# Cross-attention and quantised feed-forward on one core: probabilities in 64-column chunks, the rests as 32-row tiles

## The chip, the cores and the metric

The kernel runs on one core of a Trainium2 chip. The metric is device microseconds of one execution, the median of three runs. Engines are named as the profile names them: PE multiplies matrices (PEld is its weight load), DVE, ACT and POOL work elementwise, SP issues DMAs.

## The reference, cut to what matters

```python
x = x + attention(layernorm(x), ctx, Wq, Wk, Wv, Wo, bo)     # x (8, 512, 512), ctx (8, 77, 384)
x = x + ffn(layernorm(x), clip_x, clip_h, w_gate, w_up, w_down)

def attention(x, c):               # 8 heads of 64, L = 77 context rows
    q, k, v = split(x @ Wq), split(c @ Wk), split(c @ Wv)
    attn = softmax(einsum('bhsd,bhld->bhsl', q, k) * 64 ** -0.5)
    return merge(einsum('bhsl,bhld->bhsd', attn, v)) @ Wo + bo

def ffn(x):                        # one scale for the whole of x, one for the whole of h, one per weight row
    xq = fake_quant(x, clip_x)
    h = fake_quant(silu(xq @ quant(w_gate).T) * (xq @ quant(w_up).T), clip_h)
    return h @ quant(w_down).T
```

Because the scale of x is a maximum over all rows, no row enters the feed-forward part before attention has ended for all of them.

## The kernel before, in words

There are eight batches of 512 rows (index b) and 32 tiles of 128 rows (index n or s, s = 4b + t). The first stage is attention, and beside it the weights of the feed-forward part are turned into integers. The second and third stages are the two feed-forward products; the change touches neither.

Each engine has one queue. The order of calls in the code is the order in each queue, and each call names tokens (semaphore and value) that its engine waits for; nothing behind a waiting instruction of that engine starts before it. Matrix products of the attention stage that need more than bfloat16 split each operand into a high and a low part and add three products, high by high, high by low, low by high, of 32-bit words ("f32" in the rows). So one product over 128 contraction rows is three PE instructions of 512 columns.

`attend(s)` is one step of the loop over tiles. In it stand, for different tiles: `S(s+1)`, the scores, eight PE instructions into the two SP banks; `soft_max`, `soft_sub` (DVE), `soft_exp` (ACT), `soft_sum`, `soft_rec` (DVE) and `soft_norm` (POOL), the softmax of tile s+1, which leaves probabilities of 8 heads x 77 columns = 616 columns in `P`, a ring of three; `PT(s)`, five transposes of 128 columns to the PTP banks, then `PT_high` (ACT) and `PT_low` (DVE), which leave the transposed probabilities, high and low, in `pts` as five chunks of 128 contraction rows by 512; `wo(s-5)`, twelve PE instructions of the output product into the bank WOP, and `residual(s-5)` (DVE), which reads WOP and adds x; `second_stats`, `second_aggr`, `second_scale`, `normed` and `largest`, the second layernorm and the running maximum; `first_stats(s+3)` to `first_bias(s+3)`, the first layernorm's figures; `q_chunk`, twelve PE instructions each, four chunks a batch, which use the two QO banks in turn.

One feed-forward weight tile goes through each step: `w_load(s)` (SP, into `wraw`, two buffers), `w_top(s-1)` (a DVE maximum), `w_scale`, `w_inverse`, `w_round(s-1)` (ACT), `w_integer(s-1)` (POOL), `w_turn(s-2)` (PE transposes into the bank MI) and `w_out(s-2)` (ACT, out of MI). `w_turn` waits for the last reader of MI, whose token is `t_we["last"]`.

Every fourth step (t = 0, b >= 1) also holds the product of probabilities and V of batch b-1, `PV(b-1, j)` for the head pairs j = 0..3. Heads of 77 rows don't line up with chunks of 128, so a pair of heads meets two chunks: there are eight blocks (chunk, pair), listed in `BLOCKS`, each 128 rows by 128 columns of V in `vbd` with zeros where the other head's rows lie. PV(b, j) is six PE instructions into a QO bank, and one ACT and one DVE instruction (L200, L202) read the bank and leave the high and low part in `os_`. `load_vb(b)` fills `vbd` for batch b from a scratch in HBM in twelve DMAs on SP. It waits for the last PV of the batch before (`t_PV`). It stands in attend(4b), behind the store of x1 and the load of x, ahead of everything that attend(4b+1) issues on SP.

The order of a step with t = 0 is written out by hand (L659 to L697): `first_stats`, `w_top`, `first_aggr`, `w_scale`, `wo`, `residual`, `w_inverse`, PV 0, second statistics, PV 1, S, `soft_max`, `soft_sub`, PV 2, `soft_exp`, PT, `largest`, `soft_sum`, `soft_rec`, PV 3, `load_vb`, `PT_high`, `PT_low`. After the loop the last batch's PV comes behind `wo(27)` and `residual(27)` (L861 to L872), and `wo(28)` to `wo(31)` follow, each head pair of `wo(28)` as soon as its part of `os_` is there.

Of the kernel before, what the change touches and what calls it, by code (L numbers as in the profile page):

```python
# [54 lines left out]
def block_kernel(nc, x, xT, ctxT, Wq, Wk, Wv, Wo, bo, clip_x, clip_h, w_gate, w_up, w_down, out):  # L55
    f32, f32r, bf16 = mybir.dt.float32, mybir.dt.float32r, mybir.dt.bfloat16
    ALU, ACT, AX = mybir.AluOpType, mybir.ActivationFunctionType, mybir.AxisListType
    NB, L, H, D, I = 8, 77, 8, 512, 1408
    NT, NI = 32, 11
    HL = H * L  # L60
# [5 lines left out]
    with ctx:  # L66
# [75 lines left out]
        UR = 3  # L142
        P = sb(late, "P", [128, UR, 640])
        qs = sb(late, "qs", [128, 2, 4, 512])
# [5 lines left out]
        n2 = sb(late, "n2", [128, RR, D])  # L150
        vbd = sb(late, "vbd", [128, 2, 8, 128], f32r)
        pts = sb(late, "pts", [128, 2, 5, 512], f32r)
# [171 lines left out]
        t_bn1, t_q, t_oss, t_st2, t_wmx, t_wsc = [Tokens() for _ in range(6)]  # L324

        def q_chunk(b, m):
            w = slice(m * 128, m * 128 + 128)
            pairs = [(wqs[:, 0, k, w], wqs[:, 1, k, w], xTs[:, 0, k, :], xTs[:, 1, k, :])
                     for k in range(4)]
            at, bank, t_qh[b, m] = qo_bank(pairs, 512, 128, [*t_wql, *t_xTs[b]])  # L330
            t_q[b] = copy("act", qs[:, b % 2, m, :], bank,
                          [t_qh[b, m], t_S.get(4 * (b - 2) + 3), t_ctxl, *t_wql], "q_out")
            state["free"][at] = (t_q[b],)

        BLOCKS = [(0, 0), (1, 0), (1, 1), (2, 1), (2, 2), (3, 2), (3, 3), (4, 3)]

        def load_vb(b):
            at = 0
            while at < HL:
                hh, l0, ch, p0 = at // L, at % L, at // 128, at % 128  # L340
                n = min(L - l0, 128 - p0)
                blk = BLOCKS.index((ch, hh // 2))
                t = dma("sp", vbd[p0:p0 + n, :, blk, (hh % 2) * 64:(hh % 2) * 64 + 64],
                        vd[b * L + l0:b * L + l0 + n, :, hh * 64:hh * 64 + 64],
                        [t_v[(b * L + L - 1) // 128], t_v[b * L // 128], t_PV.get(b - 1), t_vb["zero"]], "ld_vb")
                at += n
            t_vb[b] = t
# [23 lines left out]
        def soft_sub(n):  # L371
# [19 lines left out]
        def soft_norm(n):  # L391
            u = P[:, n % UR, 0:HL].rearrange("p (h l) -> p h l", h=H)
            rb = rs8[:, n % 2, :].unsqueeze(2).broadcast_to([128, H, L])
            t_norm[n] = add("pool", lambda e: e.tensor_tensor(u, u, rb, ALU.mult), [t_rec[n]], "sm_nrm")  # L394

        def PT(n):
            b, t = n // 4, n % 4

            def fn(e):
                for k in range(5):  # L400
                    m = e.transpose(PTP[:, k * 128:k * 128 + 128], P[:, n % UR, k * 128:k * 128 + 128],  # L401
                                    identF[:, :])
                return m
# [9 lines left out]
        def PT_low(n):  # L413
            w = slice(n % 4 * 128, n % 4 * 128 + 128)
            t_pl[n] = less("dve", pts[:, 1, :, w], PT_src, pts[:, 0, :, w], [t_ph[n]], "PT_lo")

        def PV(b, j):
            pairs = [(vbd[:, 0, i, :], vbd[:, 1, i, :], pts[:, 0, ch, :], pts[:, 1, ch, :])
                     for i, (ch, jj) in enumerate(BLOCKS) if jj == j]
            last = qo_product(pairs, 512, 128, [t_pl[4 * b + 3], t_vb[b]], lambda bank: [  # L420
                (bank, os_[:, 0, j, :], os_[:, 1, j, :])], [t_Wo.get(4 * b - 1)] + t_flat)
            t_oss[b, j] = last[1]
            t_PV[b] = ("qo_mm", c.count["qo_mm"])

# [202 lines left out]
        def attend(s):  # L627
# [31 lines left out]
            if t == 0:  # L659
# [14 lines left out]
                if s > 0:
                    S(s + 1)
                    soft_max(s + 1)
                    soft_sub(s + 1)
# [492 lines left out]
```

How the kernel before makes its waits and increments, by code:

```python
    def run(self, engine, e):  # L39
        for need, fn, sem, by in self.queue[engine]:
            for s, v in need:
                e.wait_ge(s, v)
            ins = fn(e)
            if sem is not None:
                ins.then_inc(sem, by)
```

## Time and profile before

| what | us |
|---|---|
| median of three runs | 599.78 (599.04 to 600.22) |
| profiled execution, its own time | 599.7 |
| its span | 597.9 |
| PE busy in the span | 560.9 |
| DVE busy in the span | 492.2 |
| attention stage, from the start to about | 328 |

The profiled execution's own time is 1.8 us over its span, and 0.1 us under the median. A PE instruction's end in the profile is modelled, 0.39 us after the start for 512 columns, while the next one starts 0.23 us after it: starts are to be read, not busy time.

### The profile page before, as it was taken

To read this page: it belongs to the slowest core of one execution; us is meant where nothing else is said; L and a number is where in the kernel's file an instruction comes from. 1 tells how busy PE (TensorE), PEld (TensorE's weight loads), DVE (VectorE), ACT (ScalarE), POOL (GpSimd) and SP (SyncE) were. 2 spreads that over 40 slices of the span, in tenths; PEclk is the share of its full clock that TensorE was granted. 3 is DMA by queue.
4 is the path that set the end of the run, shared out by engine and by line. 5 is a ranking of instruction groups with operands and counts; after the bars stand their busy time and mean duration, and the time that the engine had idled before them with its cause. 6 is when DMAs were issued, how large, how long until landed. Compare 5 with 4: busy or idle time off the path is not lost.

```text
span 597.9 us, 8609 instructions
## 1 busy us (share of the span) xinstructions
PE 560.9 (94%) x2919; PEld 381.9 (64%) x2943; DVE 492.2 (82%) x873; ACT 327.5 (55%) x466; POOL 254.6 (43%) x321
## 2 busy tenths in 40 slices
PE   4999799999999999999989899999999999778996
PEld 2987578888888888888878644444444446333342
DVE  3747876888979797887986699889988988899994
ACT  4743456456665655655342566656665635993210
POOL 3656847658576585755532000000000000476764
PEclk9999899999999999999999999999999999999999
DMA  8617254846466573625257906532020200299975
GB/s 321 217 70 268 62 168 136 273 116 192 167 210 233 161 214 118 210 72 182 81 182 285 345 18 265 197 138 72 1 70 2 70 2 1 84 289 323 325 246 175
DMA packets 68476, 98.04 MB, mean 164 GB/s; under 512 B 31977, under 2 KB 31977, under 8 KB 67921
## 3 DMA queue, kind: packets, MB, share of 16 engines
q1 hardware_dynamic: 68429, 97.50, 49.2%
q8 instruction: 23, 0.38, 0.3%
q14 instruction: 20, 0.16, 0.1%
q10 hardware_dynamic: 4, 0.00, 0.0%
HBM read 59.70 MB, written 37.78 MB: 163 GB/s over the span
## 4 chain that ended last, share of the span: by engine, by line
PE 61%; issue 11%; DVE 11%; DMA 7%; POOL 4%; SPq 3%; ACT 2%; DVEq 0%; POOLq 0%; ACTq 0%
PE SP L972 10%; PE QO L972 10%; PE QO L183 7%; PE QO L185 6%; PE QO L184 6%; PE SP L356 4%; SPq L37 3%; PE WOP L435 3%; PE WOP L437 3%; PE WOP L436 3%; POOL n2b L1090 3%; DMA out<-n2b 2%; DVE wgu L1049 2%; PE PTP L401 2%; DVE wgu L1058 2%
## 5 line engine op out<-in xcount | busy, mean ns | idle before, releaser
L1090 POOL TENSOR_TENSOR n2b<-n2b 128x512 f32<-128x512 f32 x31 | 54.0, 1757 | 208.3 <-DVE n2b L1088 208.3
L972 PE MATMUL SP<-nT,wgu 128*128 128x512 bf16 x345 | 89.8, 379 | 0.4
L972 PE MATMUL QO<-nT,wgu 128*128 128x512 bf16 x343 | 88.7, 379 | 1.2 <-ACT nT L210 0.8
L978 ACT ACTIVATE sil<-QO,fsc 128x512 f32<-128x512 f32 x88 | 60.7, 689 | 50.5 <-PE QO L972 44.9
L982 DVE SCALAR_TENSOR_TENSOR h<-SP,fsc,sil 128x512 f32<-128x512 f32 x88 | 65.9, 749 | 14.9 <-PE SP L972 14.9
L394 POOL TENSOR_TENSOR P<-P,rs 128x616 f32<-128x616 f32 x32 | 39.0, 1219 | 73.7 <-DVE rs L388 73.6
L1046 ACT ACTIVATE h<-h,magic,g 128x1536 f32<-128x1536 f32 (+2 forms) x38 | 48.7, 1365 | 28.1 <-DMA h<-h_spill 24.4
L985 DVE TENSOR_REDUCE hmx<-h 128x1 f32<-128x512 f32 x88 | 60.4, 686 | 3.0
L972 PEld LDWEIGHTS SP<-nT,wgu 128*128 128x128 bf16 x352 | 34.4, 98 | 41.5
L183 PE MATMUL QO<-xTs,wqs 128*128 128x512 f32 x128 | 52.5, 410 | 4.2 <-POOL xTs L214 2.7
L972 PEld LDWEIGHTS QO<-nT,wgu 128*128 128x128 bf16 x352 | 33.2, 98 | 35.4 <-ACT nT L210 0.7
L185 PE MATMUL QO<-xTs,wqs 128*128 128x512 f32 x128 | 50.8, 397 | 0.0
L184 PE MATMUL QO<-xTs,wqs 128*128 128x512 f32 x128 | 50.5, 394 | 0.0
L435 PE MATMUL WOP<-wos,os 128*128 128x512 f32 x116 | 46.4, 400 | 0.0
L437 PE MATMUL WOP<-wos,os 128*128 128x512 f32 x116 | 45.3, 391 | 0.0
L436 PE MATMUL WOP<-wos,os 128*128 128x512 f32 x116 | 45.2, 389 | 0.0
L379 ACT ACTIVATE P<-P,r 128x616 f32<-128x616 f32 x32 | 26.0, 812 | 33.2 <-DVE P L375 33.1
L456 POOL TENSOR_TENSOR xn<-xn,bob 128x512 f32<-128x512 f32 x32 | 41.3, 1295 | 0.0
L356 PE MATMUL SP<-kst,qs 128*128 128x154 f32 x256 | 39.9, 298 | 0.3 <-DVE P L375 0.3
L544 ACT ACTIVATE wraw<-wraw,magic,wiv 128x512 f32<-128x512 f32 (+1 forms) x26 | 24.3, 933 | 28.5 <-DVE wiv L537 28.5
L200 ACT ACTIVATE os<-QO 128x512 fp32r<-128x512 f32 x32 | 19.2, 599 | 36.8 <-PE QO L185 36.8
L1058 DVE TENSOR_SCALAR wgu<-wgu 128x1536 bf16<-128x1536 bf16 (+2 forms) x39 | 37.4, 973 | 0.0
(163 smaller groups left out, 1265.4 us busy)
## 6 DMA issues: line engine op xcount, KB each, us to landing
xTr<-in_xT SPq DMA_DIRECT2D x8, 1024.0 KB, 6.8
xn<-in_x SPq DMA_DIRECT2D x32, 256.0 KB, 4.0
x_rows<-x SPq DMA_DIRECT2D x32, 256.0 KB, 3.2
n_rows<-n SPq DMA_DIRECT2D x32, 256.0 KB, 2.5
n2b<-n_rows SPq DMA_DIRECT2D x32, 256.0 KB, 4.1
n2b<-x_rows SPq DMA_DIRECT2D x32, 256.0 KB, 4.2
out<-n2b SPq DMA_DIRECT2D x32, 256.0 KB, 3.2
h_spill<-h SPq DMA_DIRECT2D x2, 2816.0 KB, 9.6
```

What stands on the lines that cost most here:

```text
L183: e.matmul(ps, lh, rh, start=(i == 0), stop=False)
L184: e.matmul(ps, lh, rl, start=False, stop=False)
L185: m = e.matmul(ps, ll, rh, start=False, stop=(i == n - 1))
L356: m = e.matmul(o, qs[:, b % 2, j, w], kst[:, b, j, :], start=(j % 2 == 0), stop=True, skip_group_check=True)
L435: e.matmul(wo_bank(n), os_[:, 0, j, w], wos[:, 0, j, :], start=(j == 0), stop=False)
L436: e.matmul(wo_bank(n), os_[:, 0, j, w], wos[:, 1, j, :], start=False, stop=False)
L437: return e.matmul(wo_bank(n), os_[:, 1, j, w], wos[:, 0, j, :], start=False, stop=(j == 3))
L972: m = e.matmul(ps, wv_[:, k, col:col + 128], nT[:, b % 2, k, :], start=(k == 0), stop=(k == 3))
L978: t_sil[n] = add("act", lambda e: e.activation(sil[:, n % SR, :], gp, ACT.Silu, scale=fsc[:, ic:ic + 1]), [t_g[n], t_fs, t_h.get(n - SR)] ...
L982: t_h[n] = add("dve", lambda e: e.scalar_tensor_tensor(out=hv, in0=up, scalar=fsc[:, 11 + ic:12 + ic], in1=sil[:, n % SR, :], op0=ALU.mult ...
L985: t_hm[n] = add("dve", lambda e: e.tensor_reduce(hmx[:, n:n + 1], hv, AX.X, ALU.max, apply_absolute_value=True), [t_h[n]], "hmx")
L1090: t_oa[m] = add("pool" if m < NT - 1 else "dve", lambda e: e.tensor_tensor(xo[:, so, :], xo[:, so, :], xo[:, m % 4, :], ALU.add), [t_om[m] ...
```

## The change

What it does:

- The normalised probabilities no longer overwrite `P`; `soft_norm` writes them to a new tile `PN`, two buffers of 640 columns, in two POOL instructions: columns 0 to 63 of each head at pitch 64 (four chunks of 128, one for each head pair), and the other 13 of each head at pitch 16 (the fifth chunk: 32 rows for each head pair).
- `vbd` has five blocks: four of 128 rows (one for each head pair) and one in which head pair j has rows 32j to 32j+31. `load_vb` issues two DMAs a head, sixteen in all.
- The product is a new function `PV_rest(b)`, twelve PE instructions with 32 contraction rows each, the four head pairs in turn, into four banks (the two QO banks, MI, WOP), and then `PV(b, j)` with three PE instructions of 128 rows that add to bank j. `PV_rest` waits for the four banks: the two QO ones, the last reader of MI, and `residual(4b-1)` as the reader of WOP.
- The reader of head pair 2's bank becomes `t_we["last"]`, for which the next `w_turn` waits. `wo(n)` of the first tile of a batch waits for all four parts of `os_` before its first instruction.
- In a step with t = 0, S, `soft_max` and `soft_sub` go ahead of `PV_rest` and PV 0, `soft_exp` behind PV 0, `soft_sum` and `soft_rec` ahead of PV 3, and PT and `largest` behind PV 3.

```diff
-        P = sb(late, "P", [128, UR, 640])
+        P = sb(late, "P", [128, UR, HL])
+        PN = sb(late, "PN", [128, 2, 640])
-        vbd = sb(late, "vbd", [128, 2, 8, 128], f32r)
+        vbd = sb(late, "vbd", [128, 2, 5, 128], f32r)
...
+        M0 = 64
+        M1 = L - M0
         def load_vb(b):
...
+            for hh in range(H):
+                c0, j = hh % 2 * 64, hh // 2
+                for p0, blk, l0, l1 in ((c0, j, 0, M0), (16 * hh, 4, M0, L)):
+                    t = dma("sp", vbd[p0:p0 + l1 - l0, :, blk, c0:c0 + 64],
+                            vd[b * L + l0:b * L + l1, :, hh * 64:hh * 64 + 64], waits, "ld_vb")
...
         def soft_norm(n):
-            rb = rs8[:, n % 2, :].unsqueeze(2).broadcast_to([128, H, L])
-            t_norm[n] = add("pool", lambda e: e.tensor_tensor(u, u, rb, ALU.mult), [t_rec[n]], "sm_nrm")
+            for at, l0, l1, pitch in ((0, 0, M0, 64), (512, M0, L, 16)):
+                to = PN[:, n % 2, at:at + H * pitch].rearrange("p (h l) -> p h l", h=H)[:, :, 0:l1 - l0]
+                rb = rs8[:, n % 2, :].unsqueeze(2).broadcast_to([128, H, l1 - l0])
+                t_norm[n] = add("pool", lambda e, to=to, rb=rb, l0=l0, l1=l1: e.tensor_tensor(
+                    to, u[:, :, l0:l1], rb, ALU.mult), [t_rec[n], t_PT.get(n - 2), t_pz], "sm_nrm")
...
+        def PV_rest(b):
+            banks = []
+            for j in range(2):
+                at = state["use"] % 2
+                state["use"] += 1
+                banks.append((at, state["banks"][at], state["free"][at]))
+            banks.append((None, MI[:, :], (t_we["last"], *t_dgs[1:])))
+            banks.append((None, WOP[:, :], (t_x1.get(4 * b - 1),)))
+            pv_at[b] = banks
+            def fn(e):
+                for i, (hv, hp) in enumerate(((0, 0), (0, 1), (1, 0))):
+                    for j in range(4):
+                        q = slice(32 * j, 32 * j + 32)
+                        m = e.matmul(banks[j][1], vbd[q, hv, 4, :], pts[q, hp, 4, :], start=(i == 0), stop=False)
+                return m
+            add("pe", fn, [t_pl[4 * b + 3], t_vb[b], *(t for bank in banks for t in bank[2])], "qo_mm")
+
         def PV(b, j):
+            at, bank, _ = pv_at[b][j]
+            def fn(e):
+                e.matmul(bank, vbd[:, 0, j, :], pts[:, 0, j, :], start=False, stop=False)
+                e.matmul(bank, vbd[:, 0, j, :], pts[:, 1, j, :], start=False, stop=False)
+                return e.matmul(bank, vbd[:, 1, j, :], pts[:, 0, j, :], start=False, stop=True)
+            t_PV[b] = add("pe", fn, [], "qo_mm")
...
+            if j < 2:
+                state["free"][at] = (t_oss[b, j],)
+            elif j == 2:
+                t_we["last"] = t_oss[b, j]
...
-                t_Wo[n] = add("pe", fn, [t_oss[b, j], t_wol, free, t_c], "Wo_mm")
+                t_Wo[n] = add("pe", fn, [t_oss[b, 3 if t == 0 else j], t_wol, free, t_c], "Wo_mm")
...
                 when("w", w_inverse, s - 1)
+                if s > 0:
+                    S(s + 1)
+                    soft_max(s + 1)
+                    soft_sub(s + 1)
+                when("pv", PV_rest, b - 1)
                 when("pv", PV, b - 1, 0)
+                if s > 0:
+                    soft_exp(s + 1)
                 when("wo", second_stats, s - 5)
                 when("wo", second_aggr, s - 5)
                 when("wo", second_scale, s - 5)
                 when("pv", PV, b - 1, 1)
                 when("pv", PV, b - 1, 2)
+                when("s", soft_sum, s + 1)
+                when("s", soft_rec, s + 1)
+                when("pv", PV, b - 1, 3)
...
                 PT(s)
                 when("am", largest, s - 7)
-                when("s", soft_sum, s + 1)
-                when("s", soft_rec, s + 1)
-                when("pv", PV, b - 1, 3)
...
         second_stats(27)
+        PV_rest(7)
         PV(7, 0)
```

## Rows read from the trace of the kernel before

**Rows 1.** The page, its first part: busy time, share of span, instructions.

```profile
PE 560.9 (94%) x2919; PEld 381.9 (64%) x2943; DVE 492.2 (82%) x873; ACT 327.5 (55%) x466; POOL 254.6 (43%) x321
```

**Rows 2.** Busy time by window: PE, PEld, DVE, ACT, POOL, granted clock, DMA share.

```profile
182.40:217.00 34.60, 34.52 (x192) 29.13 (x192) 30.41 (x60) 20.66 (x32) 23.39 (x34) 1.00 0.62 196
```

**Rows 3.** Waits, attention stage: engine, line, releaser, us in total, times, longest.

```profile
DVE wmx L528 <- DMA wraw<-in_ffn_w_gate: 10.5, 4, 3.0
```

**Rows 4.** Timeline 181.5 to 193, PE and PEld: start, us (merged), instruction.

```profile
182.44 0.39 PE L183 MATMUL QO<-pts,vbd 128*128 128x512 f32 x1
182.66 0.39 PE L184 MATMUL QO<-pts,vbd 128*128 128x512 f32 x1
...
184.93 1.20 PEld L356 LDWEIGHTS SP<-kst,qs 128*128 128x128 f32 x8
185.16 1.21 PE L356 MATMUL SP<-kst,qs 128*128 128x154 f32 x8
186.10 0.49 PE L183 MATMUL QO<-pts,vbd 128*128 128x512 f32 x1
...
187.60 0.71 PE L401 MATMUL PTP<-identF,P 128*128 128x128 f32 x5
...
189.54 0.40 PE L564 MATMUL MI<-identB,wint 128*128 128x128 bf16 x4
```

**Rows 5.** The same timeline, DVE and ACT around residual(11) and PV.

```profile
182.44 0.69 DVE L442 BATCH_NORM_STATS2 bn<-xn 128x6 f32<-128x512 f32 x1 [0.69 <-DMA xn<-in_x]
...
183.86 0.69 DVE L461 TENSOR_TENSOR x<-WOP,xn 128x512 f32<-128x512 f32 x1
...
184.00 0.60 ACT L200 ACTIVATE os<-QO 128x512 fp32r<-128x512 f32 x1 [1.32 <-PE QO L185]
...
184.63 0.69 DVE L202 TENSOR_TENSOR os<-QO,os 128x512 fp32r<-128x512 f32 x1
...
185.23 0.68 DVE L467 BATCH_NORM_STATS2 bn<-x 128x6 f32<-128x512 f32 x1
...
185.95 0.18 DVE L471 BATCH_NORM_AGGREGATE mv<-bn 128x2 f32<-128x6 f32 x1
186.05 0.66 DVE L202 TENSOR_TENSOR os<-QO,os 128x512 fp32r<-128x512 f32 x1
...
186.63 0.79 DVE L368 TENSOR_REDUCE mx<-SP 128x8 f32<-128x616 f32 x1
```

**Rows 6.** The tile vbd: duration ns min/median/max, first and last start.

```profile
L37 SPq DMA_DIRECT2D vbd<-v_halves x96: 613/795/955, 64.1 to 302.0; - x96
```

**Rows 7.** Timeline of SP: V loads and the weight load behind them.

```profile
64.13 9.86 SPq L37 DMA_DIRECT2D vbd<-v_halves  x12
...
189.77 9.79 SPq L37 DMA_DIRECT2D vbd<-v_halves  x12
...
200.77 0.65 SPq L37 DMA_DIRECT2D wraw<-in_ffn_w_up  x1
```

**Rows 8.** Timeline of DVE, from w_top(17) to residual(15).

```profile
204.14 0.69 DVE L528 TENSOR_REDUCE wmx<-wraw 128x1 f32<-128x512 f32 x1 [2.76 <-DMA wraw<-in_ffn_w_up]
...
206.62 0.69 DVE L461 TENSOR_TENSOR x<-WOP,xn 128x512 f32<-128x512 f32 x1 [0.83 <-PE WOP L437]
...
218.63 0.69 DVE L461 TENSOR_TENSOR x<-WOP,xn 128x512 f32<-128x512 f32 x1
```

**Rows 9.** Timeline, the first PV and what DVE waits for there.

```profile
75.74 0.47 PE L183 MATMUL QO<-pts,vbd 128*128 128x512 f32 x1 [0.97 <-DMA vbd<-v_halves]
...
77.50 0.69 DVE L528 TENSOR_REDUCE wmx<-wraw 128x1 f32<-128x512 f32 x1 [3.03 <-DMA wraw<-in_ffn_w_gate]
```

**Rows 10.** Timeline, the steps in which batch 6 and batch 7 get their PV.

```profile
287.08 0.69 DVE L461 TENSOR_TENSOR x<-WOP,xn 128x512 f32<-128x512 f32 x1
...
293.81 0.49 PE L435 MATMUL WOP<-wos,os 128*128 128x512 f32 x1
...
311.68 0.69 DVE L461 TENSOR_TENSOR x<-WOP,xn 128x512 f32<-128x512 f32 x1 [1.08 <-PE WOP L437]
...
317.30 0.39 PE L435 MATMUL SP<-wos,os 128*128 128x512 f32 x1
```

More of the change, by code:

```diff
@@ L324, in block_kernel @@
         t_bn1, t_q, t_oss, t_st2, t_wmx, t_wsc = [Tokens() for _ in range(6)]
+        t_dgs = []
         def q_chunk(b, m):
@@ L333, in q_chunk @@
             state["free"][at] = (t_q[b],)
-        BLOCKS = [(0, 0), (1, 0), (1, 1), (2, 1), (2, 2), (3, 2), (3, 3), (4, 3)]
+        M0 = 64
+        M1 = L - M0
         def load_vb(b):
[L338 to L346, printed above, removed]
+            waits = [t_v[(b * L + L - 1) // 128], t_v[b * L // 128], t_PV.get(b - 1), t_vb["zero"]]
+            for hh in range(H):
[3 more added lines that the diff above has]
+                            vd[b * L + l0:b * L + l1, :, hh * 64:hh * 64 + 64], waits, "ld_vb")
             t_vb[b] = t
@@ L375, in soft_sub @@
             t_sub[n] = add("dve", lambda e: e.tensor_tensor(u, S4, mb, ALU.subtract),
-                           [t_mx[n], t_PT.get(n - UR), t_wkl, t_ctxl], "sm_sub")
+                           [t_mx[n], t_norm.get(n - UR), t_wkl, t_ctxl], "sm_sub")
         def soft_exp(n):
@@ L400, in fn @@
                 for k in range(5):
-                    m = e.transpose(PTP[:, k * 128:k * 128 + 128], P[:, n % UR, k * 128:k * 128 + 128],
+                    m = e.transpose(PTP[:, k * 128:k * 128 + 128], PN[:, n % 2, k * 128:k * 128 + 128],
                                     identF[:, :])
@@ L415, in PT_low @@
             t_pl[n] = less("dve", pts[:, 1, :, w], PT_src, pts[:, 0, :, w], [t_ph[n]], "PT_lo")
-        def PV(b, j):
[L418 to L423, printed above, removed]
+        pv_at = {}
+        def PV_rest(b):
[14 more added lines that the diff above has]
+            add("pe", fn, [t_pl[4 * b + 3], t_vb[b], *(t for bank in banks for t in bank[2])], "qo_mm")
+        def PV(b, j):
+            at, bank, _ = pv_at[b][j]
[4 more added lines that the diff above has]
+            t_PV[b] = add("pe", fn, [], "qo_mm")
+            hi, lo = os_[:, 0, j, :], os_[:, 1, j, :]
+            waits = [t_Wo.get(4 * b - 1)] + t_flat
+            th = add("act", lambda e: e.activation(hi, bank, ACT.Copy), [t_PV[b], *waits], "qo_hi")
+            t_oss[b, j] = add("dve", lambda e: e.tensor_tensor(lo, bank, hi.bitcast(f32), ALU.subtract),
+                              [th, *waits], "qo_lo")
+            if j < 2:
+                state["free"][at] = (t_oss[b, j],)
+            elif j == 2:
+                t_we["last"] = t_oss[b, j]
         def wo_bank(n):
@@ L431, in wo @@
             w = slice(t * 128, t * 128 + 128)
-            free = t_x1.get(n - 1) if n < 28 else (t_sub[31], None, t_x1[27], t_pl[31])[n - 28]
+            free = t_x1.get(n - 1) if n < 28 else (t_sub[31], None, t_oss[7, 3], t_pl[31])[n - 28]
             for j in range(4):
@@ L597, in block_kernel @@
         t_wol = less("pool", wos[:, 1], wor[:, :, :], wos[:, 0], [t_woh], "wo_lo")
-        t_pz = add("pool", lambda e: e.memset(P[:, :, HL:640], 0.0), [t_ctxl, t_wkl], "c_pz")
+        t_pz = add("pool", lambda e: e.memset(PN[:, :, 512:640], 0.0), [t_ctxl, t_wkl], "c_pz")
         v_rows(0)
@@ L673, in attend @@
                 when("pv", PV, b - 1, 1)
[L674 to L677, printed above, removed]
                 when("pv", PV, b - 1, 2)
-                if s > 0:
-                    soft_exp(s + 1)
+                when("s", soft_sum, s + 1)
+                when("s", soft_rec, s + 1)
+                when("pv", PV, b - 1, 3)
                 if big:
```

1 line of the change is left out of this document (removed).

## The prediction, made before the changed kernel ran

> **What bounds the kernel now.** I read the page's busy times first [rows 1]: PE 560.9 of 597.9 us. Busy PE time is modelled, so I went to a window of one batch in the attention stage [rows 2]: PE 34.5 of 34.6 us, DVE 30.4, at full clock (1.00, the 2.4 GHz level). The timeline by starts says the same [rows 4]: 512-column products start 0.227 us apart without a gap. PE sets the pace of this stage, and a batch's PV is 24 such starts, 24 x 0.227 = 5.45 us. The waits then show what lies close behind PE [rows 3]: DVE waits 10.5 us in four times for weight tiles, and for the other weight another three times. In each batch one `w_top` stands idle 2.5 to 2.8 us [rows 8], because its load leaves SP only behind the twelve V loads, 9.8 us of issuing [rows 7]. So DVE has some 4 us of idle time a batch, and nearly three of them hang on SP, not on PE.
>
> **The change part by part.** I call G the end of the residual that releases WOP: 183.86 + 0.69 = 184.55 for s = 16 [rows 5].
>
> *PE work.* 24 starts become 12 full ones, 12 x 0.227 = 2.72 us, and 12 with 32 rows, which I call R. No row shows tiles of 32 rows. Below: the four banks' tiles run together, three slots, 3 x 0.227 = 0.7 us. Above: they run one by one with a hand-over at each end, 2.72 + 0.2 = 2.9 us (the hand-over is the 0.33 against 0.23 us by which a product after scores starts late, in the same timeline). Between lies the weight load: the scores load 128 columns of 32-bit weights for each of eight instructions and start 0.94/8 = 0.118 us apart with far fewer columns to stream [rows 4]. Twelve tiles bring twelve such loads, 12 x 0.118 = 1.4 us. I take 1.4, since it is the only row with as many loads for as little streaming. PE alone would then save 5.45 - 2.72 - 1.4 = 1.3 us a batch.
>
> The Trainium skill (TensorE: Matmul & The Clock Gate, measured speedup of packing) gives 3.07 times for four tiles of 32 rows and 512 columns; by that R would be 2.72/3.07 = 0.9, an estimate, and the sum about 3.5 us lower. Its page TensorEngine Tiling (Array Packing), key properties, says that a change of tiling mode drains the array, which speaks against the change at both ends of the twelve. No row of this trace shows either.
>
> *The new wait for WOP.* `PV_rest` waits for G. Before, PV began at 182.44, as soon as wo(11) had been issued [rows 4]. Now scores fill 0.95 us of it, to 183.39, and then PE stands until 184.61: 1.2 us. Residual is late because DVE has `first_stats` (0.69 us waiting for x), `w_top` and two small ones in front of it [rows 5]. G minus the start of PV in the six batches with a residual is 3.3, 1.6, 2.1, 1.35, 0.9 and 2.1 us, and 0.9 at the end, where nothing fills it. Behind the waiting instruction on PE stand all of PV, PT, `w_turn` and the next scores.
>
> *The new wait for MI.* `w_turn` now waits for the DVE reader of head pair 2. From the start of PV 0: 0.84 to its third product's end, 0.04 and 0.60 for ACT, 0.03, so DVE's first reader starts at 1.51; then by starts 0.60, 0.72, 0.10 (reader, statistics, aggregate), 0.58, and the third reader's 0.69 [rows 5] with a handover: about 4.3 us, while PE needs 2.72 + 0.55 for the rest of PV and PT. So `w_turn` starts at G + 0.06 + R + 4.3 = G + 5.8, here 190.3, against 189.54 before. PE's saving of 1.3 has become a loss of 0.8 us in this batch.
>
> *Four more V loads.* Issue time hardly depends on the rows of a piece: 0.61 to 0.96, median 0.80 us [rows 6]; a piece of 25 rows takes 0.72. Four more at 0.72 are 2.9 us; low end 1.7 (all sixteen like the shortest kinds), high end 3.4. SP's next weight load goes out so much later, and DVE already waits for it.
>
> *One batch round.* From G to the next G by way of SP and DVE, at s = 16: 0.06 + R 1.4 + 2.72 + 0.21 to PV's end (4.39); V loads and what follows to the landing of the weight tile, 204.14 - 189.77 = 14.37 before [rows 7, 8], plus 2.9; DVE from `w_top` to the next residual's end, 219.32 - 204.14 = 15.18 less the 0.83 us in which it waits for PE [rows 8], which vanish: 14.35. Sum 36.0, before 219.32 - 184.55 = 34.8: +1.2. The other four rounds repeat the pattern with their own figures: s = 8 to 12, 36.2 against 34.3, +1.9; 12 to 16, 36.3 against 35.8, +0.5; 20 to 24, 35.2 against 34.8, +0.4; 24 to 28, which has fewer q products, 33.1 against 33.6, -0.5. There PE's own way, 0.06 + 1.4 + 4.3, then 25.3 us of PE work unchanged, then 2.1, gives the same 33.1. Together +3.5 us.
>
> *The first PV.* PE already waits 0.97 us for V [rows 9]: twelve issues from 64.13 [rows 7] set it. With sixteen V is there 2.9 us later, about 78.7, and the weight tile behind them too, so that `w_top` starts near 80.5 instead of 77.50 [rows 9]. `soft_max` and `soft_sub` now stand between it and the readers: they end about 83.2, the third reader about 85.9, and `w_turn`, at 82.91 before, starts at 86: +3.0 us. The scores moved ahead only fill a wait.
>
> *The last two.* At s = 28 there is no `w_turn`, but wo(24) waits for all four readers. With sum and reciprocal ahead of the fourth it is G + 0.06 + 1.4 + 5.8 = 295.0 (G = 287.77) against 293.81 [rows 10]: +1.2. After the loop: G = 312.37; PV 0 at 313.8, first reader 315.3, then aggregate, two readers, `largest`, the fourth until 318.5; wo(28) at 318.6 against 317.30 [rows 10]: +1.3. Before, nine products of wo(28) covered the last reader; now nothing does.
>
> *At nothing.* `soft_norm` in two POOL instructions costs at most some 0.1 us each time; POOL has 11 us free a batch [rows 2], and PT comes a step later. Zeroing is shorter. S moved ahead: its softmax comes earlier, nobody waits for it. The three-deep `P` is released earlier, which nobody needed. If POOL's cover were gone, 32 x 0.1 = 3 us.
>
> **Sum.** 3.0 + 3.5 + 1.2 + 1.3 = +9.0 us. On the profiled execution's 599.7 (span 597.9 and 1.8 around it) that is 608.7; the median of the runs shown is 0.1 above that execution.
>
> **The rivals.**
>
> *The saving comes through (faster).* Place: the wait for WOP. If residual kept pace, because PE's waits give DVE time to catch up, and the V loads' issue stayed hidden, each of eight PVs would keep 2.72 - 1.4 = 1.3 us: 599.7 - 10.5 = 589.2. It decides where G comes within 0.95 us of the end of wo, as in one batch of seven. Against it: DVE's wait for the weight tile [rows 8] is in its own queue and grows with SP's work whatever PE does.
>
> *Cheap tiles, cheap issues (no change).* R = 0.7 and 1.7 us for the V loads. Then PE's way binds: rounds +0.7, -0.5, 0, -0.7, -1.2, first PV +1.8, last two +0.5 and +0.6, in sum +1.2: 600.9.
>
> *The tiles don't run together.* The change doesn't do what it says, R = 2.9. Each of the five rounds and the last two get 1.5 longer, the first hardly: 608.7 + 10.5 = 619.2. For it: no row shows tiles side by side. Against: they go to different banks and different rows.
>
> **How the numbers follow.** Forecast 55%, its own range 604 to 613 (R from 0.9 to 2, issues 2.4 to 3.4 us). Saving 14%, cheap 17%, one by one 14%. Less than 0.2% (1.2 us) can't be told from no change. Cheap splits evenly over faster, same and slower; faster 0.19, same 0.07, slower 0.74. The range 598 to 619 leaves out most of the saving case and the top of the one-by-one case.
>
> **What would show it.** Right: the twelve 32-row tiles spanning about 1.4 us; PE idle before them, released by the residual; PE idle before `w_turn`, released by the DVE reader; sixteen V issues of 12.7 us; DVE's four waits for the one weight, 10.5 us [rows 3], grown to over 16; a batch round near 36 us; PE idle of 1 to 2 us before wo(28). Wrong: tiles in under 0.8 us, a residual that ends within a microsecond of wo, DVE waits for weight tiles as before, or a batch round under 34 us.

## The result, and the profile after

| | median us | lowest to highest | profiled span | mean granted clock |
|---|---|---|---|---|
| before | 599.41 | 598.66 to 600.22 | 597.9 | 0.996 |
| after | 609.85 | 609.62 to 610.27 | 608.3 | 0.988 |

The changed kernel is slower: ratio 1.0175, 95% interval 1.0157 to 1.0192. The span grew by 10.4 us; the forecast was +9.0, 608.7 us.

The page of after, busy times first (answers to [rows 1]). PE is busy 1.8 us less in a span that is 10.4 us longer, so its share fell from 94% to 92%: what PE was spared, and more, came back as waits (and a stretch at half the clock, below, counts as busy).

```profile
PE 559.1 (92%) x2943; PEld 372.6 (61%) x2943; DVE 491.7 (81%) x873; ACT 324.1 (53%) x466; POOL 258.7 (43%) x353
```

The waits of after between 20 and 355 us (engine, line, releaser, total us, times, longest) name the new ones: `w_turn` waits for the reader that frees MI, `PV_rest` for the residual that frees WOP, wo(28) (bank SP) and wo(24) (bank WOP) for the fourth reader. DVE still waits for weight tiles, 11.1 us in three times where [rows 3] had 10.5 in four.

```profile
PE MI L599 <- DVE os L453: 7.7, 6, 3.2
PE QO L438 <- DVE x L496: 4.8, 6, 2.1
...
PE SP L470 <- DVE os L453: 1.9, 1, 1.9
PE WOP L470 <- DVE os L453: 1.3, 1, 1.3
...
DVE wmx L563 <- DMA wraw<-in_ffn_w_gate: 11.1, 3, 4.9
DVE wmx L563 <- DMA wraw<-in_ffn_w_up: 9.7, 3, 3.3
```

One batch's PV at s = 16, from the timeline of after (start, us, instruction), stands against [rows 4, 5]. The first four tiles, in four banks, start within 0.01 us of each other, and so do their weight loads. The next fours start 0.30 to 0.34 and 0.23 us later, and the first full product 0.32 to 0.36 after the last four: R = 192.63 - 191.73 = 0.90 us. Then 12 products, PT, and PE stands until the third reader (196.26 + 0.68) has freed MI.

```profile
190.89 0.69 DVE L496 TENSOR_TENSOR x<-WOP,xn 128x512 f32<-128x512 f32 x1
...
191.73 0.50 PE L438 MATMUL QO<-pts,vbd 32*128 32x512 f32 x2 [0.18 <-DVE x L496]
191.74 0.18 PEld L438 LDWEIGHTS MI<-pts,vbd 32*128 32x128 f32 x1
191.74 0.49 PE L438 MATMUL MI<-pts,vbd 32*128 32x512 f32 x1
191.74 0.18 PEld L438 LDWEIGHTS WOP<-pts,vbd 32*128 32x128 f32 x1
191.74 0.49 PE L438 MATMUL WOP<-pts,vbd 32*128 32x512 f32 x1
...
192.04 0.39 PE L438 MATMUL QO<-pts,vbd 32*128 32x512 f32 x1
...
192.27 0.39 PE L438 MATMUL QO<-pts,vbd 32*128 32x512 f32 x1
...
192.63 0.50 PE L446 MATMUL QO<-pts,vbd 128*128 128x512 f32 x1
...
195.48 0.71 PE L405 MATMUL PTP<-identF,PN 128*128 128x128 f32 x5
196.26 0.68 DVE L453 TENSOR_TENSOR os<-MI,os 128x512 fp32r<-128x512 f32 x1
197.09 0.38 PE L599 MATMUL MI<-identB,wint 128*128 128x128 bf16 x4 [0.91 <-DVE os L453]
```

SP of after, then DVE of after (against [rows 7] and [rows 8]). Sixteen V loads take 12.15 us, the weight load goes out at 209.06, and DVE waits 3.10 us for its tile. The wait is hardly longer than before, although the load is later, because everything behind the V loads moved along.

```profile
195.72 12.15 SPq L37 DMA_DIRECT2D vbd<-v_halves  x16
...
209.06 0.66 SPq L37 DMA_DIRECT2D wraw<-in_ffn_w_up  x1
```

```profile
212.26 0.69 DVE L563 TENSOR_REDUCE wmx<-wraw 128x1 f32<-128x512 f32 x1 [3.10 <-DMA wraw<-in_ffn_w_up]
...
214.32 0.69 DVE L496 TENSOR_TENSOR x<-WOP,xn 128x512 f32<-128x512 f32 x1 [0.41 <-PE WOP L472]
...
226.83 0.69 DVE L496 TENSOR_TENSOR x<-WOP,xn 128x512 f32<-128x512 f32 x1
```

The first PV of after (against [rows 9]). DVE waits 4.85 us for a weight tile; `soft_max`, `soft_sub` and the readers stand behind it, and PE waits 3.24 us for MI. After that wait PE runs with starts 0.43 us apart instead of 0.23.

```profile
79.81 0.69 DVE L563 TENSOR_REDUCE wmx<-wraw 128x1 f32<-128x512 f32 x1 [4.85 <-DMA wraw<-in_ffn_w_gate]
...
85.22 0.59 PE L599 MATMUL MI<-identB,wint 128*128 128x128 bf16 x4 [3.24 <-DVE os L453]
...
88.62 0.63 PE L186 MATMUL QO<-xTs,wqs 128*128 128x512 f32 x1
...
89.05 0.63 PE L184 MATMUL QO<-xTs,wqs 128*128 128x512 f32 x1
```

Busy time of after in that stretch (PE, PEld, DVE, ACT, POOL, granted clock): the clock is 0.50, the 1.2 GHz level, for these 5.7 us, in which PE is busy all the time. I call this a slow stretch. In windows of 0.25 us it begins at 84.5, while PE still stands, and ends at about 91.4.

```profile
85.50:91.20 5.70, 5.70 (x20) 4.93 (x19) 4.92 (x8) 1.82 (x3) 3.23 (x4) 0.50 0.15 32
```

The end of the attention stage in after (against [rows 10]): PE waits for WOP, and then 1.92 us for wo(28)'s fourth reader.

```profile
321.42 0.50 PE L438 MATMUL QO<-pts,vbd 32*128 32x512 f32 x2 [0.88 <-DVE x L496]
...
327.28 0.50 PE L470 MATMUL SP<-wos,os 128*128 128x512 f32 x1 [1.92 <-DVE os L453]
```

**Where the 10.4 us came from.** I call G, as in the prediction, the end of the residual in front of a batch's PV, and add up by G. First PV and the round behind it, up to s = 8: 119.71 against 114.43, +5.3. From s = 8 to the last G: 201.57 against 197.94, +3.6. From there to the end: 287.01 against 285.54, +1.5. G is an event on DVE. After's PV waits for it; the PV of before doesn't, and there G comes 0.9 to 3.3 us behind the start of PV. So G splits the whole, but a single round of before can differ from the round that PE sees.

### The profile page after: what moved, and what is told of

It is laid out like the page before. It is cut to its first block, busy times and chain, and to the rows that moved or that the text cites. A ratio compares the mean times of both kernels' runs of the same rounds, so it can differ in the third digit from the quotient of the medians.

```text
span 608.3 us, 8706 instructions
## 1 busy us (share of the span) xinstructions
PE 559.1 (92%) x2943; PEld 372.6 (61%) x2943; DVE 491.7 (81%) x873; ACT 324.1 (53%) x466; POOL 258.7 (43%) x353
## 4 chain that ended last, share of the span: by engine, by line
PE 51%; DVE 15%; issue 13%; POOL 8%; DMA 6%; ACT 3%; SPq 3%; POOLq 0%; DVEq 0%; ACTq 0%
PE QO L1007 10%; PE SP L1007 10%; POOL n2b L1125 5%; PE QO L184 4%; PE QO L186 4%; PE QO L185 4%; SPq L37 3%; PE SP L357 3%; PE WOP L470 2%; PE WOP L471 2%; PE WOP L472 2%; DVE os L453 2%; DMA xn<-in_x 2%; DVE x L496 1%; DMA n2b<-x_rows 1%
## 5 line engine op out<-in xcount | busy, mean ns | idle before, releaser
L1007 PE MATMUL QO<-nT,wgu 128*128 128x512 bf16 x352 | 90.3, 379 | 0.6 <-ACT nT L211 0.6
L397 POOL TENSOR_TENSOR PN<-P,rs 128x512 f32<-128x512 f32 x64 | 44.2, 712 | 64.1 <-DVE rs L389 64.1
L184 PE MATMUL QO<-xTs,wqs 128*128 128x512 f32 x128 | 53.3, 417 | 4.6 <-POOL xTs L215 2.7
L186 PE MATMUL QO<-xTs,wqs 128*128 128x512 f32 x128 | 51.4, 402 | 0.0
L185 PE MATMUL QO<-xTs,wqs 128*128 128x512 f32 x128 | 51.3, 400 | 0.0
L470 PE MATMUL WOP<-wos,os 128*128 128x512 f32 x116 | 46.9, 405 | 1.3 <-DVE os L453 1.3
L471 PE MATMUL WOP<-wos,os 128*128 128x512 f32 x116 | 45.8, 395 | 0.0
L472 PE MATMUL WOP<-wos,os 128*128 128x512 f32 x116 | 45.8, 394 | 0.0
L563 DVE TENSOR_REDUCE wmx<-wraw 128x1 f32<-128x512 f32 (+1 forms) x26 | 21.0, 809 | 20.7 <-DMA wraw<-in_ffn_w_gate 11.1
L357 PEld LDWEIGHTS SP<-kst,qs 128*128 128x128 f32 x256 | 36.5, 194 | 1.6 <-DVE P L376 0.8
```

The lines of the kernel that those rows point to most:

```text
L184: e.matmul(ps, lh, rh, start=(i == 0), stop=False)
L185: e.matmul(ps, lh, rl, start=False, stop=False)
L186: m = e.matmul(ps, ll, rh, start=False, stop=(i == n - 1))
L357: m = e.matmul(o, qs[:, b % 2, j, w], kst[:, b, j, :], start=(j % 2 == 0), stop=True, skip_group_check=True)
L470: e.matmul(wo_bank(n), os_[:, 0, j, w], wos[:, 0, j, :], start=(j == 0), stop=False)
L471: e.matmul(wo_bank(n), os_[:, 0, j, w], wos[:, 1, j, :], start=False, stop=False)
```

## The experiments

The table has every run. G(8) is G at s = 8, "six rounds" goes from it to the last G (before the PV of batch 7), "rest" from there to the end of the span; these three are of the profiled execution (that of e2_mi0 took 601.8 us, at the low end of its runs). The ratio is against the kernel before on the same chip (599.62, 599.65 and 599.49 us beside e1 to e4, e5 to e8 and e9 to e12).

| kernel | V loads a batch | median us | ratio (95%) | G(8) | six rounds | rest |
|---|---|---|---|---|---|---|
| before | 12 | 599.41 | 1 | 114.43 | 197.94 | 285.54 |
| after | 16 | 609.85 | 1.0175 (1.0157 to 1.0192) | 119.71 | 201.57 | 287.01 |
| e1_v12 | 12 | 599.45 | 0.9997 (0.9987 to 1.0007) | 112.32 | 198.17 | 288.54 |
| e2_mi0 | 16 | 604.86 | 1.0084 (1.0065 to 1.0104) | 113.02 | 200.00 | 287.02 |
| e3_full | 16 | 620.63 | 1.0341 (1.0324 to 1.0359) | 116.69 | 211.90 | 290.35 |
| e4_b16 | 16 | 618.29 | 1.0309 (1.0295 to 1.0323) | 119.25 | 211.89 | 285.49 |
| e5_before_spread | 12 in four | 639.84 | 1.0662 (1.0647 to 1.0676) | 114.92 | 232.52 | 290.45 |
| e6_after_spread | 16 in four | 633.78 | 1.0569 (1.0545 to 1.0593) | 121.18 | 222.33 | 291.38 |
| e7_spread_mi0 | 16 in four | 629.93 | 1.0491 (1.0461 to 1.0521) | 116.00 | 219.89 | 292.93 |
| e8_spread_all | 16 in four | 627.07 | 1.0438 (1.0407 to 1.0468) | 112.38 | 222.99 | 289.71 |
| e9_before_half | 12 in two | 598.75 | 0.9989 (0.9980 to 0.9997) | 113.75 | 197.21 | 285.53 |
| e10_after_half | 16 in two | 603.47 | 1.0076 (1.0056 to 1.0096) | 114.65 | 197.70 | 288.57 |
| e11_half_mi0 | 16 in two | 596.02 | 0.9947 (0.9935 to 0.9959) | 112.83 | 192.52 | 288.52 |
| e12_half_all | 16 in two | 590.57 | 0.9855 (0.9842 to 0.9868) | 111.71 | 191.76 | 286.25 |

### One part at a time

**e1_v12**: the kernel after without the four loads it adds; the last 13 rows of the odd heads are left out.

```diff
-                for p0, blk, l0, l1 in ((c0, j, 0, M0), (16 * hh, 4, M0, L)):
+                for p0, blk, l0, l1 in ((c0, j, 0, M0), (16 * hh, 4, M0, L))[:2 - hh % 2]:
```

> The changed kernel with twelve V loads a batch instead of sixteen (the rests of the four odd heads are left out, so their last 13 context rows count as zero). My theory: the four extra issues are on the path of DVE (the weight tile's load stands behind them); without them the rounds shrink until PE's own way binds, some 0.9 us in each of five, and the first PV and the clock drop behind it get 2 us shorter: about 604 us. Rival, that only PE's waits for banks matter: within 1 us of 609.9.

Measured: 599.45, no difference from before, 4.6 us below the theory's 604; the rival is out. So the four loads carry the whole loss, 10.4 us, and the rest of the change comes to zero: what PE saves it gives back. The two new waits of this kernel, with the 1.93 us before wo(28), show 9.6 us of that. DVE's waits for the one weight are down to 4.1 us, 2.7 of them at the first PV:

```profile
PE MI L599 <- DVE os L453: 5.1, 6, 0.9
...
PE QO L438 <- DVE x L496: 2.6, 4, 1.1
...
DVE wmx L563 <- DMA wraw<-in_ffn_w_gate: 4.1, 4, 2.7
```

Not all of the 10.4 us is the longer block of loads itself. After's slow stretch behind the first PV, some 2.8 us (see e3_full), is missing here: the granted clock is 1.00 from 85.5 to 91.2. On the other side this kernel has a slow stretch behind wo(28) that after hasn't, in the windows of e1_v12 and then of after:

```profile
316.50:319.75 3.25, 3.25 (x8) 2.57 (x9) 0.51 (x1) 0.00 (x0) 0.00 (x0) 0.52 0.80 292
```

```profile
327.30:330.50 3.20, 3.20 (x14) 2.60 (x15) 0.64 (x2) 0.00 (x0) 0.00 (x0) 1.00 0.84 274
```

wo(28) starts 5.99 and 6.01 us after the last G in the two, but the next PE instruction that waits (L938) comes at 23.79 against 22.26. These 1.5 us are why the column "rest" is 288.5 here. e10_after_half and e11_half_mi0 have the same slow stretch and the same 1.5 us, and e3_full has it beside its longer PV. Why the clock falls there in four kernels and not in after and e2_mi0, which stand as long before wo(28), no run shows.

**e2_mi0**: MI goes to the first head pair instead of the third, so that its reader comes first.

```diff
-            banks.append((None, MI[:, :], (t_we["last"], *t_dgs[1:])))
+            banks.insert(0, (None, MI[:, :], (t_we["last"], *t_dgs[1:])))
...
-            if j < 2:
+            if 1 <= j <= 2:
                 state["free"][at] = (t_oss[b, j],)
-            elif j == 2:
+            elif j == 0:
                 t_we["last"] = t_oss[b, j]
```

> The changed kernel with MI given to head pair 0 instead of pair 2, whose DVE reader comes first, so w_turn's wait ends some 2 us earlier. If the wait for MI is on the path: PE's gap of 1.07 us before w_turn goes in five batches, the 3.4 us one at the first PV shrinks, and the half clock behind it (3 us) goes: about 600. If SP's V loads and DVE set the rounds, only the first PV and the clock get better: about 605. If neither: 609.9.

Measured: 604.86 (601.83 to 606.06), 5.0 us less than after, as the middle case had it. The parts can be read only for the profiled execution, which took 601.83, 8.2 us less than after's. Its rounds gain only 1.6 us: the wait for MI is gone, and others stand in its place, of which these are the largest.

```profile
PE QO L184 <- DVE xTs L215: 2.8, 5, 1.9
PE PTP L405 <- DVE pts L215: 2.5, 6, 1.3
PE MI L599 <- POOL wint L585: 2.1, 4, 1.1
```

The larger gain is before s = 8: G(8) is 6.7 us earlier. Its `w_turn` at the first PV starts at 82.28 instead of 85.22, after a wait of 0.54 instead of 3.24, and from 82.20 to 92.00 the granted clock stays at 1.00:

```profile
82.28 0.38 PE L599 MATMUL MI<-identB,wint 128*128 128x128 bf16 x4 [0.54 <-DVE os L453]
```

```profile
82.20:92.00 9.80, 9.72 (x57) 8.43 (x58) 9.04 (x16) 6.24 (x11) 4.64 (x6) 1.00 0.36 117
```

5.7 us at half the clock cost after about 2.85 us, an estimate; with the 2.9 by which `w_turn` is earlier that is 5.8 of the 6.7.

**e3_full**: the 12 rest tiles as full instructions of 128 rows, in four blocks of their own.

```diff
-                        q = slice(32 * j, 32 * j + 32)
-                        m = e.matmul(banks[j][1], vbd[q, hv, 4, :], pts[q, hp, 4, :], start=(i == 0), stop=False)
+                        m = e.matmul(banks[j][1], vbd[:, hv, 4 + j, :], pts[:, hp, 4, :], start=(i == 0), stop=False)
```

> The changed kernel with the twelve 32-row tiles as twelve full 128-row instructions (V's rests in four blocks with zeros), all else as it is. The tiles take 0.90 us a batch in the trace, twelve full starts would take 2.72. If PE's way is on the path: +1.8 us x 8, about 623. If the tiles' saving is hidden behind SP and DVE: under +5, below 615.

Measured: 620.63, +10.8 us over after. The twelve tiles became 2.80 to 2.85 us instead of 0.90; from first to last start a PV takes 5.32 instead of 3.53, so it is 1.8 us longer eight times, 14.3 us. A round got 1.7 us longer on average (211.90 - 201.57 over six), so a microsecond of PV is on the path nearly whole. What is missing to 14.3 lies before s = 8, where G came 3.0 us earlier than in after: here PE stands only 1.42 us before `w_turn` at the first PV, and the slow stretch of after is missing.

```profile
84.95 0.38 PE L598 MATMUL MI<-identB,wint 128*128 128x128 bf16 x4 [1.42 <-DVE os L452]
```

```profile
84.00:90.00 6.00, 5.05 (x29) 4.41 (x30) 5.93 (x9) 3.53 (x6) 3.26 (x4) 1.00 0.29 91
```

This run also prices that stretch. From `w_turn` to G at s = 8, where the two kernels do the same work behind the same sixteen loads, it takes 31.74 us (116.69 - 84.95), after 34.49 (119.71 - 85.22), before 31.5: the stretch costs after some 2.8 us.

**e4_b16**: the kernel before, with four of its pieces of 77 rows cut into 64 and 13. Same data and PE work, 16 loads.

```diff
-                t = dma("sp", vbd[p0:p0 + n, :, blk, (hh % 2) * 64:(hh % 2) * 64 + 64],
...
+                for r0, r1 in ((0, 64), (64, 77)) if n == 77 else ((0, n),):
+                    t = dma("sp", vbd[p0 + r0:p0 + r1, :, blk, (hh % 2) * 64:(hh % 2) * 64 + 64],
```

> The kernel before with four of its twelve V pieces of 77 rows cut in 64 and 13, so sixteen V loads a batch, same data. My theory: the issues cost by themselves about 2 us at the first PV, and in the rounds they only lengthen DVE's wait for the weight tile from 2.7 to 5 us, of which PE sees little, since it doesn't wait for the residual: 601.5 to 604. Rival, that the V loads alone explain the change: about 610.

Measured: 618.29, +18.7 us. This is the miss that taught most. I had taken DVE's idle time for slack of PE in the kernel before; four loads, 2.5 us of issuing, made a batch 1.4 to 3.3 us longer by G in each of five rounds, and G(8) 4.8 later. By the starts of PV on PE, the better measure for this kernel, the first two PVs are 3.0 and 6.5 us later than before, and the five rounds 1.8, 2.6, 4.1, 2.5 and 1.2 us longer: at most places no more than the 2.5 us of issuing. The 4.1 holds a slow stretch (below), and another, from 79.7 to 83 us, lies in the first PV behind a wait of 2.58 us for V. SP of this kernel, the w_top behind it, and its waits:

```profile
200.66 12.24 SPq L37 DMA_DIRECT2D vbd<-v_halves  x16
...
214.13 0.64 SPq L37 DMA_DIRECT2D wraw<-in_ffn_w_up  x1
```

```profile
217.49 0.69 DVE L530 TENSOR_REDUCE wmx<-wraw 128x1 f32<-128x512 f32 x1 [5.21 <-DMA wraw<-in_ffn_w_up]
...
233.11 0.69 DVE L463 TENSOR_TENSOR x<-WOP,xn 128x512 f32<-128x512 f32 x1 [0.82 <-PE WOP L439]
```

```profile
PE PTP L403 <- DVE pts L214: 5.4, 6, 1.2
...
DVE wmx L530 <- DMA wraw<-in_ffn_w_gate: 21.4, 5, 5.8
DVE wmx L530 <- DMA wraw<-in_ffn_w_up: 15.5, 3, 5.2
```

The late weight tile makes `w_top` late, with it everything behind it on DVE, and in the fourth step `PT_low`, for which PE's next PT waits. In the round from s = 16 PE stands 1.16, 0.35 and 0.23 us there, and behind these short waits the granted clock is 0.50 from about 226.5 to 229.8:

```profile
224.05 0.74 PE L403 MATMUL PTP<-identF,P 128*128 128x128 f32 x5 [1.16 <-DVE pts L214]
```

```profile
226.50:229.75 3.25, 3.25 (x9) 2.48 (x9) 3.22 (x9) 0.69 (x1) 3.09 (x5) 0.50 1.00 307
```

`w_top` to G takes 1.1 us longer than before in this round, and 0.2 longer in the one ahead of it, which has no slow stretch. One round, from G at s = 16 to the next, split alike in three kernels (before from [rows 5, 7, 8]):

| | G to first V issue | V issues | to w_top | w_top to next G | round |
|---|---|---|---|---|---|
| before | 5.22 | 9.79 | 4.58 | 15.18 | 34.77 |
| e4_b16 | 4.96 | 12.24 | 4.59 | 16.31 | 38.10 |
| after | 4.13 | 12.15 | 4.39 | 15.26 | 35.93 |

So a ring runs through all three: PV, V loads (they wait for PV), weight tile, DVE, PV. In after its last link is the residual, for which `PV_rest` waits. In before and e4_b16 PV doesn't wait for the residual, and the last link is `PT_low`, for which PT waits. In e4_b16 the ring sets the rounds. In before PE does (PE waits 0.2 us in all for `PT_low`, and e9_before_half below loosens the ring without gain), but the ring has almost nothing to spare, so that 2.5 us of issuing came through whole. After is 8.4 us faster than e4_b16 at the same 16 loads; that it is the shorter PV is shown by e3_full, which lacks only that and is at 620.63. So the change gains 8.4 us at 16 loads, nothing at 12, and its four loads cost more.

### The loads taken out of the way

**e5_before_spread, e6_after_spread**: three (four) V loads at the end of each of the four steps, instead of one block.

```diff
-                if 1 <= b < NB:
-                    load_vb(b)
...
+            if b >= 1:
+                load_vb(b, t)
```

> The kernel before with its twelve V loads a batch spread over the four steps, three in each, instead of in a block ahead of the weight tile's load. Theory (the block of V loads is what DVE waits behind, and only a longer block reaches PE): DVE's wait of 2.5 to 2.8 us a batch goes, PE was never idle, so within 1.5 us of 599.6. Rival (PE-side: DVE's slack feeds back into the rounds already before): 3 us faster or more.

> The changed kernel with its sixteen V loads spread over the four steps, four in each; the first batch's sixteen stay in one block. If the block is what costs, not the number of loads: as with twelve loads (599.5), plus 1 to 3 us for the first PV, so 599 to 603. If the number of loads on SP costs wherever they stand: above 606.

Measured: 639.84 and 633.78, far off. I had looked only at the loads behind the V loads, not at the reader of the last quarter. It goes out just before its own PV. SP and PE of e5_before_spread:

```profile
195.18 2.45 SPq L37 DMA_DIRECT2D vbd<-v_halves  x3
...
199.37 0.47 PE L183 MATMUL QO<-pts,vbd 128*128 128x512 f32 x1 [4.12 <-DMA vbd<-v_halves]
...
200.44 0.63 PE L183 MATMUL QO<-pts,vbd 128*128 128x512 f32 x1
200.86 0.63 PE L184 MATMUL QO<-pts,vbd 128*128 128x512 f32 x1
```

PE stands 4.12 us and then again runs with starts 0.42 to 0.43 us apart, at a granted clock of 0.50 from 200 to 203 us. Both come back with each batch: by G the five rounds of e5_before_spread are 39.6 to 42.3 us long. **e7_spread_mi0** has the edit of e2 as well, **e8_spread_all** also the two further edits of e12 below.

> The changed kernel with the V loads spread and MI given to head pair 0. With the V loads out of the way PE's wait for MI (1.07 us in each of five rounds, more at the first PV) should be real time: 5 to 6 us below the kernel with the loads spread alone, about 595. If something else steps in as it did behind the block of loads, where the wait only moved to the third step: within 2 us of it.

> The last one with two more waits shortened: the residual first in DVE's order of a step with t = 0, so that PV_rest waits less for WOP (0.35 to 2.3 us in six batches), and wo(28) taking each head pair's part as it comes (2.1 us of wait before, 1.3 of it new). If these are PE time: 4 to 6 us below the last one, about 590; if DVE's other work sets the rounds then: within 2 us of it.

Measured: 629.93 and 627.07, 3.9 and 2.9 us below the one before each, where 5 to 6 and 4 to 6 had been expected. The wait for the last V loads is in both, so they say little about the kernel without it.

**e9_before_half to e12_half_all**: V loads in two halves, the first where the block stood, the second one step later behind `x_in`; two steps are left until PV.

```diff
-                    load_vb(b)
+                    load_vb(b, 0)
...
                 x_in()
+                if t == 1 and b >= 1:
+                    load_vb(b, 1)
```

e9 has only this on the kernel before, e10 only this on the kernel after, e11 adds the edit of e2, e12 adds two more: residual first in DVE's order of the step, and wo(28) waits for its head pairs one by one.

```diff
+                when("wo", wo, s - 5)
+                when("wo", residual, s - 5)
                 when("x", first_stats, s + 3)
...
-                when("wo", wo, s - 5)
-                when("wo", residual, s - 5)
...
-                t_Wo[n] = add("pe", fn, [t_oss[b, 3 if t == 0 else j], t_wol, free, t_c], "Wo_mm")
+                t_Wo[n] = add("pe", fn, [t_oss[b, 3 if t == 0 and n < 28 else j], t_wol, free, t_c], "Wo_mm")
```

> The kernel before with its V loads in two halves, six where the twelve stood and six in the next step behind the load of x, so that weight tiles and V are both in time. DVE's waits of 2.5 to 2.8 us a batch for the weight tile should go. PE never waited for them before: 597.5 to 599.6. If DVE's slack mattered before: 2 us faster or more.

> The changed kernel with its sixteen V loads in two halves of eight in the same two places (the first batch's stay in one block). If the block ahead of the weight tile sets the rounds, they shrink from 35.9 to some 34.9 us as with twelve loads, while the first PV's wait and the half clock behind it stay (5 us): about 605. If the number of loads counts wherever they stand: 609 or more.

> The last one with MI given to head pair 0. Behind the block of loads this took the wait before w_turn away and DVE made up a new one in the third step. With the loads in halves it should be real: 1.07 us in each of five rounds, and 3 to 5 us at the first PV, where the gap of 3.4 us and the half clock go: about 596. If the wait moves again: 601 or more.

> The last one with the residual first in DVE's order of a step with t = 0 and with wo(28) taking each head pair's part as it comes. PE's waits for WOP (0.35 to 1.5 us in six batches) and before wo(28) (2.1 us) shrink: 3 to 5 us below the last one, about 592, and below the kernel before with the same load order. If DVE sets the rounds by then: within 2 us of the last one.

Measured: 598.75, 603.47, 596.02, 590.57, each within 1.6 us of the theory's figure. On the kernel before the order of loads is worth 0.1%, on the changed kernel 6.4 us: there the ring was binding. The profiled executions lie 7.4 us apart; 3.9 of them are in the six rounds and 4.9 between `w_turn` at the first PV (85.02 against 85.22) and s = 8, and the slow stretch behind wo(28) takes 1.5 back. Of the 4.9 some 2.8 are after's slow stretch, which had been expected to stay; though PE stood 2.81 us for MI, the clock behind it is 1.00 in this execution. It may not be so in each: three runs of e10_after_half took 602.5 to 602.7 us at a mean granted clock of 0.989 to 0.991, three 604.2 to 606.8 at 0.985 or 0.986.

With the ring loosened PE still waits for MI in each batch (7.3 us in e10_after_half), and now the edit of e2 is worth 7.5 us: the three waits that took its place behind the block of loads are not among the long ones of e11_half_mi0. Residual first and wo(28) give 5.5 more, 4.1 in the profiled executions. Of these 1.1 come before s = 8, 0.8 in the six rounds and 2.3 behind them: with the wait before wo(28) gone, the slow stretch behind it is gone too, and up to the PE instruction L940 this saves 3.65 us (G + 20.15 against G + 23.80); part of it is lost again in the feed-forward stage, where this trace has 7.0 us at the lower clock and that of e11_half_mi0 3.5. In e12_half_all a whole round has PE busy from end to end (window of s = 16), and the long waits for weight tiles are down to one:

```profile
179.70:213.60 33.90, 33.90 (x196) 28.29 (x195) 30.01 (x62) 21.48 (x33) 24.61 (x40) 1.00 0.64 201
```

```profile
DVE wmx L563 <- DMA wraw<-in_ffn_w_gate: 3.6, 1, 3.6
```

This version beats both kernels: 1.45% under before (interval 1.32% to 1.58%), 8.2 us under the kernel before with the same order of loads. By starts a PV takes 3.76 us of PE (3.53 from first to last start and one slot of 0.23) instead of 5.45, so the tiles save 1.7 us each time, 13.5 in all, and over half of that arrives; the five rounds between the PVs of s = 8 and 28 are 1.2 to 1.4 us shorter than those of e9_before_half. No run puts the residual first in the kernel before, so what that order would be worth without the tiles isn't shown.

## Why the prediction was nearly right, step by step

- **Sign and mechanism held, the size partly by luck.** The rounds between s = 8 and 28 came out at +1.6, +0.1, +1.2, +0.5, -0.45, in sum +3.0, where the ring had given +3.5. e1_v12 and e4_b16 show what it rests on: without the four loads nothing is lost. But the four terms that the sum did price (3.0, 3.5, 1.2, 1.3) came to 2.3 + 3.0 + 0.6 + 1.5 = 7.4 us instead of 9.0, and a term that it lacked, 3.0, brought the total to +10.4.
- **The tiles**, R: 0.90 us, not 1.4. The step that failed is "twelve tiles bring twelve such loads": the weight loads of four tiles lie beside each other, as the timeline shows, and don't add up. The page of the Trainium skill named in the prediction (TensorE: Matmul & The Clock Gate, measured speedup) was right, 0.9. The drain that the Trainium skill speaks of (TensorEngine Tiling (Array Packing), key properties) can be no longer, behind the twelve, than the 0.32 to 0.36 us from the last four to the first full product, 0.1 more than the usual 0.23, about what a product after scores takes too (0.34 us, from 186.10 to 186.44 in before).
- **Four more V loads**: 12.15 against 9.79, +2.4 us, not +2.9.
- **These two errors were hidden by a third.** DVE from `w_top` to the next G was 15.26, not 14.35: I took away the whole wait for wo, 0.83, but 0.41 of it stayed, and 0.49 for `pts` came new.
- **Wait for WOP**: 0.9 us at the tail, as priced, 0.95 at s = 28 and 2.10 at s = 8; but at s = 16 only 0.18 instead of 1.2, because PE itself came later.
- **Wait for MI**: `w_turn` at G + 5.50 (197.09 - 191.59), priced at G + 5.8 with R too long by 0.5; the wait is 0.91.
- **First PV**: `w_turn` at 85.22, +2.3, priced at +3.0. What failed is the silence about what follows: the round from there to s = 8 was taken as unchanged and got 3.0 us longer. Some 2.8 of it are the slow stretch at the 1.2 GHz level, which begins while PE stands 3.2 us: e3_full, with the same loads and the clock at 1.00, takes 31.74 us for this piece, about what before takes, and after 34.49. That is the term that the sum lacked.
- **The last two**: +0.6 (25.22 against 24.60) and +1.5, priced at 1.2 and 1.3. The wait of wo(24) is there, 1.25 us at 302.97, and so are the 1.92 before wo(28).
- **Waits for the one weight "grown to over 16"**: wrong, 11.1 us. In a ring a longer load moves everything behind it, the waiter too; the wait is no measure of the loss. In e4_b16 it did grow, to 21.4.
- **soft_norm at nothing**: 1.38 against 1.22 us each time. PE waits for it in two places, 2.6 us in all against 2.4 before, so it was next to nothing.
- **The rival "the saving comes through"** was refuted for this kernel, but its two conditions could be made, with MI freed early as a third: residual first and the loads out of the way. e12_half_all is at 590.57, where that rival had 589.2. That the figures are so near is chance: the rival took tiles of 1.4 us and let the whole saving through.

Open: why the granted clock falls behind some waits and not behind others (behind wo(28) in e1, e3, e10 and e11, not in after and e2, at the same wait of 1.9 us); and why the runs of e2_mi0 reach from 601.83 to 606.06. Their mean granted clock doesn't sort them: it is 0.991 in the fastest and 0.989 to 0.994 in the others.

## What to carry to other kernels

Follow each queue once around a whole round before you call idle time slack: an engine's wait for a load can be a link of a ring that has almost nothing to spare, even where PE looks 99.8% busy [rows 2] and sets the round, and the test is cheap (add four small loads and change nothing else). A cut in PE's work pays only if the banks it takes are free, the readers that free them come first, and no queue pays for it in extra issues; here the same tiles went with nothing gained, a loss of 10.4 us, or a gain of 8.2, by the number and order of the loads and the order of the readers. And look up the clock before you explain a difference: one slow stretch cost 1.5 to 2.8 us here, as much as a term of the sum. When a block of loads is split, ask for both ends: what stands behind the first part, and when the last part is read.

## What the runs showed of the hardware

- Twelve tiles of 32 rows in four banks, 512 columns of 32-bit words, take 0.90 us; in e3_full twelve full products in their place take 2.80 to 2.85: three times less. Their weight loads start within 0.01 us of each other.
- What a V load costs SP follows its count more than its rows: with the same bytes, 16 issues took 12.24 us (e4_b16) and 12 took 9.79, so each more was 0.6 us.
- PE ran at the 1.2 GHz level after standing 3.24 us (after) and 4.12 us (e5_before_spread), with product starts 0.43 us apart instead of 0.23. In after the level began before PE did. In e10_after_half it stood 2.81 us for MI at the same place, and the granted clock behind it was 1.00.
- The longest single wait doesn't tell whether the clock falls. In e4_b16 it was 0.50 from about 226.5 to 229.8 us behind waits of 1.16, 0.35 and 0.23 us. Behind the wait of 1.9 us before wo(28) it fell in e1_v12, e3_full, e10_after_half and e11_half_mi0 (about 1.5 us lost each time), and stayed at 1.00 in after and e2_mi0.
